# Last layer of a four-layer graph network: the statistics of h behind the scans of step 16, and a softplus between the halves of a scan

## The reference

```python
h = jax.nn.relu(adj @ x @ gcn_w + gcn_b)
mu = h.mean(-1, keepdims=True)
var = h.var(-1, keepdims=True)
h = (h - mu) * lax.rsqrt(var + EPS) * ln_g + ln_b
xz = h @ w_in
xc, z = (xz[:, :D_INNER], xz[:, D_INNER:])
...
u = jax.nn.silu(xconv)
dbc = u @ w_xp
dt = jax.nn.softplus(dbc[:, :DT_RANK] @ w_dt + b_dt)
...
dA = jnp.exp(dt[:, :, None] * A[None])
dBu = dt[:, :, None] * B[:, None, :] * u[:, :, None]
def step(hst, inp):
    dAt, dBut, Ct = inp
    hst = dAt * hst + dBut
    return (hst, hst @ Ct)
_, ys = lax.scan(step, jnp.zeros((D_INNER, D_STATE), h.dtype), (dA, dBu, C))
y = ys + u * D_skip
y = y * jax.nn.silu(z)
return y @ w_out
```

## Time and profile before

| | before |
|---|---|
| median of 3 runs | 902.86 us (901.5 to 903.57) |
| profiled execution, own time | 900.57 us |
| profiled execution, span | 898.8 us |
| granted TensorE clock, mean | 0.948 |
| PE busy | 807.6 us (90%) |
| DVE busy | 691.4 us (77%) |
| ACT busy | 513.9 us (57%) |
| POOL busy | 232.3 us (26%) |

### The profile page before, as it was taken

One profiled execution on the slowest core, in us unless ns is written; L12 is line 12 of the kernel. 1 busy time (PEld: TensorE's weight loads), 2 busy tenths in 40 slices (PEclk: granted clock), 3 DMA queues, 4 the chain that ended last, 5 costly groups with the idle time before them and its releaser, 6 DMA issues. The chain is left out here.

```text
span 898.8 us, 11864 instructions
## 1 busy us (share of the span) xinstructions
PE 807.6 (90%) x4176; PEld 514.9 (57%) x4176; DVE 691.4 (77%) x994; ACT 513.9 (57%) x818; POOL 232.3 (26%) x135
## 2 busy tenths in 40 slices
PE   6999997999999999999979998998989989876665
PEld 6755545888888888884445457994332333321211
DVE  2987779999999999814873125966389899899987
ACT  2664536777777777743441116643568577676661
POOL 4000000000000000000000002001179899889993
PEclk9999998999999999999989997999999999997766
DMA  8589988210220220109810000000342715616310
GB/s 289 172 306 317 355 284 336 94 55 40 93 93 0 93 93 0 47 0 400 351 27 1 1 0 2 1 1 24 74 105 52 161 47 122 144 50 152 89 47 12
DMA packets 39264, 101.93 MB, mean 113 GB/s; under 512 B 6289, under 2 KB 11290, under 8 KB 32690
## 3 DMA queue, kind: packets, MB, share of 16 engines
q1 hardware_dynamic: 38658, 101.09, 34.4%
q10 hardware_dynamic: 560, 0.27, 0.1%
HBM read 75.87 MB, written 18.14 MB: 105 GB/s over the span
## 5 line engine op out<-in xcount | busy, mean ns | idle before, releaser
L1910 PE MATMUL PS<-big 128*128 128x256 f32 x768 | 194.4, 385 | 3.9 <-ACT big L1740 3.7
L221 PE MATMUL PS<-ident,big 128*128 128x128 f32 x1123 | 158.3, 281 | 22.3 <-DMA big<-in_L_gnn_weight 7.1
L221 PEld LDWEIGHTS PS<-ident,big 128*128 128x128 f32 x1123 | 137.1, 145 | 47.2 <-issue 21.4
L485 POOL TENSOR_TENSOR big<-big 128x1024 f32<-128x1024 f32 x63 | 147.3, 2355 | 13.3 <-DVE big L1457 8.6
L1910 PEld LDWEIGHTS PS<-big 128*128 128x128 f32 x768 | 133.7, 191 | 22.2 <-ACT big L1740 7.5
L1740 ACT ACTIVATE big<-PS 128x512 f32<-128x512 f32 x192 | 105.1, 598 | 58.2 <-PE PS L221 57.3
L440 POOL MEMSET big<- 128x16 f32 x1 | 0.1, 130 | 521.2 <-PE PS L854 521.2
L1457 DVE TENSOR_TENSOR_SCAN big<-PS,stripes,big 128x512 f32<-128x512 f32 x96 | 116.8, 1266 | 6.3 <-ACT PS L748 3.3
L2109 DVE SCALAR_TENSOR_TENSOR big<-big,rz 128x2048 f32<-128x2048 f32 x48 | 112.7, 2350 | 0.9
L2087 DVE CUSTOM_DVE_ANT_0 big<-big 128x2048 f32<-128x2048 bf16 x48 | 109.8, 2290 | 0.1
L748 ACT ACTIVATE PS<-big,stripes 128x512 f32<-128x512 f32 x128 | 86.3, 685 | 35.7 <-DVE big L1457 35.2
(11 more groups left out here) (222 smaller groups left out, 1000.3 us busy)
## 6 DMA issues: line engine op xcount, KB each, us to landing
big<-in_adj SPq DMA_DIRECT2D x16, 2048.0 KB, 9.4
big<-at_dram SPq DMA_DIRECT2D x4, 4096.0 KB, 27.9
at_dram<-big SPq DMA_DIRECT2D x3, 4096.0 KB, 16.9
big<-b_dram SPq DMA_DIRECT2D x32, 256.0 KB, 4.2
big<-big SPq DMA_DIRECT2D x24, 256.0 KB, 4.0
big<-b_dram SPq DMA_DIRECT2D x38, 128.0 KB, 3.9
at_dram<-big SPq DMA_DIRECT2D x1, 3072.0 KB, 18.7
big<-e_dram SPq DMA_DIRECT2D x3, 1024.0 KB, 6.5
```

What stands on the lines that cost most here:

```text
L221: return nc.tensor.transpose(PS[:, bank, col:col + P], src, ident[:])
L485: nc.gpsimd.tensor_tensor(dbu[k % 3], du2[c % 2][:, 2 * (n % 2):2 * (n % 2) + 2, :], bb[group % 2][:, pair_of(k) % 2, :].unsqueeze(1).to_b ...
L1910: m = nc.tensor.matmul(PS[:, 4 + k // 3, 0:256], hw[:, jt, h, :], qt[v % 4][:, 256 * c:256 * c + 256], start=(h == 0 and jt == 0), stop=(h ...
```

## The change

Two pieces of DVE's list are written elsewhere. `scan` takes a function that it calls between its two halves; in step 8 of chunks 0 to 2 that is the first softplus of the next chunk, which stood behind the whole scan. And `h_spread` of chunks 2 and 3 moves from the end of step 14 to step 15, behind the scans of the following step (16 and 32) and ahead of `weigh(15)` and `h_rescale`. No instruction is added or removed, and no other engine's list changes. After the edit the scans stand on line 1459, the weighing on line 1470, the gate product on line 1523; the lines before `scan` keep their numbers.

```diff
-            def scan(k):
+            def scan(k, between=None):
...
                 for b in range(DI):
                     j = 2 * k + b
+                    if b and between:
+                        between(c + 1, 0, 0)
                     dve.wait_ge(da_ready, j + 1)
...
                 if k + 1 < STEPS:
-                    scan(k + 1)
+                    scan(k + 1, softplus if c < NCH - 1 and n == 8 else None)
+                if c < NCH - 2 and n == 15:
+                    h_spread(c + 2, 1)
                 if not on_pool(k):
                     weigh(k)
...
-                if c < NCH - 1 and (n == 8 or n == 9):
-                    softplus(c + 1, n - 8, 0)
-                if c < NCH - 2 and n == 14:
-                    h_spread(c + 2, 1)
-                elif c < NCH - 2 and n == 15:
+                if c < NCH - 1 and n == 9:
+                    softplus(c + 1, 1, 0)
+                if c < NCH - 2 and n == 15:
                     h_rescale(c + 2, 1)
```

## The result

| | before | changed |
|---|---|---|
| median, 10 runs each, same chip | 901.88 us (897.51 to 903.57) | 906.29 us (901.77 to 910.06) |
| ratio, 95% interval | | 1.0048 [1.0028, 1.0069] |
| profiled execution, own time and span | 900.57, 898.8 us | 901.77, 900.0 us |
| mean granted TensorE clock | 0.948 | 0.942 |

The change makes the kernel slower, by 4.3 us as the ratio has it (2.5 to 6.2). The forecast of 905.8 against 902.86 was +2.96 us. The changed kernel's profiled execution is the fastest of its ten runs; the layers ahead of the edit were 3.1 us shorter in it than in the profiled execution of before: POOL's first product of the scans starts at 653.03, before at 656.14. From there to the end it is 246.97 us, before 242.66. So only the last layer can be compared, and there every stretch is counted from an instruction of the same execution.

The account below looks back on a forecast made before the run. DVE was taken to bound each chunk's first half and POOL the rest from step 24; +2.84 and +0.12 us make +2.96 on the median of 902.86, so 905.8 us, range 902.6 to 907.8.

Parts of the forecast that it names:

- The reading of who bounds what: Last layer: DVE sets the pace in a chunk's first half, POOL from step 24 on to the next chunk's first product.
- Term 1: h's statistics behind scans of steps 16 and 32: late Ln delays ACT's decay for step 17 or 33; 2 x 1.42 = +2.84 us.
- The drain: ACT's table switches at both boundaries: about 1380 ns of drain after each load; 911.3 us, chance 0.01.
- Term 2: First softplus between the halves of scans 9, 25 and 41: ACT's order eats its lead; +0.12 us, bounds -0.6 to +1.1.
- the scans fill the wait gainfully: Rival at both boundaries: DVE's waits of 1.72 and 2.01 us vanish, nothing behind ACT's Ln is late; 899.1 us, chance 0.12.
- nothing moves the end: Rival: the next chunk's first product is set by SP's transfers alone; 902.9 us, chance 0.06.
- half of the loss is absorbed: Rival: only one boundary's loss, or half of both, reaches the end; 902.86 + 1.5 = 904.4 us, chance 0.14.
- The clock's rival: TensorE's next-chunk convolution waits over 3 us, then runs 1.66 us longer per boundary at low clock; uncovered 909.1 us, chance 0.07.

Follow-up runs that it names:

- statistics alone: Against the changed kernel, the softplus goes back to its old place; only h_spread stays moved behind the scans of steps 16 and 32. 904.77 us, ratio 1.0041 against before.
- softplus alone: Against the changed kernel, h_spread goes back to step 14; only the first softplus stays between the halves of its scan. 900.56 us, ratio 0.9998 against before.
- the changed kernel again: The changed kernel measured and profiled a second time, without any further edit, beside the kernel before. 904.38 us, ratio 1.0034.

## Why the prediction was right

**The reading of who bounds what.** It held. In all of the kernels with SP's order of before, the stretches that I gave to POOL (24 to 32) took 23.25 to 23.30 us, whatever DVE did in step 9, and from step 8 to 48 the boundaries, which I gave to DVE and ACT, moved alone.

**Term 1, +2.84 us.** The statistics alone gave +1.81 and +1.46 us at the two boundaries, +3.27 in the profile, and +3.7 by the ratio (1.9 to 5.5). Each step of the working is in the rows: half 0 waits 1.14 us for POOL (forecast 1.1), the Ln waits 1.82 us (1.8), the block behind it is 4.27 us (4.27), and DVE waits 1.46 us in step 17 (1.42). Counted from the product of step 16, those of steps 32 and 48 came 1.93 and 3.44 us later, where I had 1.5 and 3.0. The second boundary fits to 0.04 us. At the first I was 0.4 us short. There the second half of step 16's scan waited 0.76 us for its decay, not 0.4, because the relu came 709.89 - 707.16 = 2.73 us after POOL's product, and in the one profile that I had 711.79 - 709.46 = 2.33. In the second changed profile, which came into step 8 without the long wait of step 7, that wait was 0.49 us and the boundary 38.40. The relu's place goes with the wait in step 7: it comes 2.33 and 2.46 us after the product in the two profiles with the short wait, and 2.67 to 2.73 in the six with the long wait and SP's order of before, whichever edit they have. Compared like with like, the first boundary lost 38.40 - 36.79 = 1.61 us where both profiles have the short wait (forecast 1.42 and 0.09 for the softplus), and 38.60 - 37.13 = 1.47 where both have the long one (statistics alone against softplus alone). So nearly all of the 0.4 us is how the one profile of before happened to lie, and little is in the term.

**The drain.** No row shows it: a load of 1.28 us, and the next instruction 1.29 or 1.30 us after its start, in this block as in the one before. The Trainium skill (page "ScalarE: Activation LUTs", section "What ACT_TABLE_LOAD costs") would have it about 1.38 us longer per switch. By that figure the loss would be 8.5 us, an estimate. The interval of the main comparison ends at 6.2, so the rows decided rightly.

**Term 2, +0.12 us, with bounds of -0.6 and +1.1.** Shown as near zero by the kernel with the softplus alone: 0.9998 [0.9977, 1.002], and 144.19 - 143.75 = 0.44 us from step 8 to 48, of which 0.34 at the first boundary. Those 0.34 are not the softplus's: the relu comes 2.67 us after the product here, before 2.33, and it comes at 2.67 with the statistics alone too, where the softplus stands in its old place. Between kernels that both have the long wait in step 7, the softplus brings 147.17 - 147.03 = 0.14 us from step 8 to 48. The mechanism that I gave, ACT's order eating the lead, is in the rows: the Abs lost its wait for TensorE (0.94 us) and the decay ahead of it got one of 1.31. In the changed kernel again, which like before had the short wait in step 7, the sum fits row by row: counted from POOL's weighing of step 9, the decay starts at -0.45 us and the Abs at +0.27, both as worked out, and the second softplus at +2.21 (2.22). In chunk 2 the second softplus waited 0.58 us, not 1.75, and the stretch 40 to 48 stayed at 23.26 us, as I had assumed.

**The rivals.** That the scans fill the wait gainfully, or that nothing moves the end, is excluded by both comparisons. That half of the loss is absorbed, 1.5 us in all, is excluded by the first interval and by the stretches: both boundaries lost, and the sum is still there at step 48. The clock's rival came true as a mechanism and cost next to nothing: the gap before the convolution was 2.60 us (I had said over 3), the four matmuls took 3.78 us, and the granted clock from 720 to 725 us was 0.57, a stretch mostly at 1.2 GHz, before 1.00. First TensorE's row in the changed kernel, then that stretch in it and in the kernel before:

```profile
720.52 3.78 PE L1037 MATMUL PS<-es,ns 128*128 128x512 f32 x4 [2.60 <-ACT es L642]
```

```profile
720.00:725.00 5.00, 4.48 (x12) 2.42 (x13) 4.65 (x5) 4.33 (x9) 4.54 (x2) 0.57 0.88 210
```

```profile
720.00:725.00 5.00, 4.50 (x24) 2.81 (x24) 4.65 (x5) 3.99 (x8) 5.00 (x3) 1.00 0.48 123
```

DVE's wait list between 721.84 and 740.98 is the same as before, one of 0.35 and one of 0.81 us, so TensorE's 1.8 us was covered.

**What is left over.** The medians moved by 4.4 us in the first comparison and 3.1 in the second, the stretches by 3.42 and 3.17. The 2.96 of the forecast lies in both intervals (2.5 to 6.2, 1.1 to 5.0), and the middle of the first is 1.3 us above it. Of that the stretches show 0.2: 3.17 us is the difference of the two profiles that both had the short wait in step 7. The rest can't be told from the scatter of single executions. That 905.8 met the measured 906.29 within 0.5 us is partly luck: over ten runs the median of before lay 0.98 us lower than over the three that the forecast started from, and the change was larger than forecast.

## What to carry to other kernels

Where an engine takes its list in order, moving the producer of a small result later delays not only its consumer but everything that stands behind the first instruction that waits for it: here a Ln of 0.3 us held 4.27 us of other work, and the decay at the end of that work was needed first. Before a wait is filled, ask of each instruction put into it what releases it: the scans that were to fill 1.72 us were themselves held 1.14 and 0.76 us by POOL and ACT. And when a late result can't be helped, the cure may be to let the one urgent instruction pass it on the waiting engine; here two decays, the urgent one and the next, were moved together, and took back the whole loss.

## What the runs showed that was not expected

From POOL's first product to its weighing of step 8, ahead of the edit, the same list of instructions takes 0.8 to 1.4 us more or less according to whether TensorE is at its low clock for some microseconds at the transposes of chunk 1. That, and the layers ahead (POOL's first product of the scans lies between 653.03 and 656.14 us in the two profiles compared), is as large as the effect under test, so a single span says nothing here. Stretches between two instructions of one execution that POOL works through repeat to 0.05 us (23.25, 23.30, 23.26, 23.28 us); a boundary, which depends on TensorE and ACT too, repeated to 0.27 us (38.67 and 38.40 in the two profiles of the changed kernel).

An idle time of POOL that the profile puts down to DVE (2.24 us before step 16's product) was SP's: with the rows of B fetched earlier it shrank, and the profile then named a DMA. In the kernel before, that product needs no later scan than step 13's, which is in this row of DVE, with step 14's:

```profile
700.25 4.70 DVE L1457 TENSOR_TENSOR_SCAN big<-PS,big 128x512 f32<-128x512 f32 x4
```

The row had ended by 700.25 + 4.70 = 704.95 us, 4.5 us ahead of the product.
